# Attention: VectorE's statistics, sums over heads and softening put between the steps of a batch's matrix

## The reference, cut to what matters

```python
q = _split_heads(x @ Wq + bq)
v = _split_heads(x @ Wv + bv)
q = jax.nn.softmax(q, axis=-1) * s
k = jax.nn.softmax(q, axis=-2) * s
ctx = jnp.einsum('bhnd,bhne->bhde', k, v)
attn = jnp.einsum('bhnd,bhde->bhne', q, ctx)
attn = attn.transpose(0, 2, 1, 3).reshape(B, N, D)
return attn @ Wo + bo
```

## Time and profile before

| | |
|---|---|
| median of 3 runs | 1755.51 us (1755.17 to 1757.69) |
| the profiled execution, its own time | 1755.51 us |
| its span, first to last instruction | 1752.8 us |
| busy over the span | TensorE 90%, VectorE 64%, ScalarE 50%, GpSimd 43% |
| attention | about 787 to 967 us |
| the three matrices of batches 0, 1 and 2 | from about 848, 892 and 933 us |

### The profile page before, as it was taken

The page is one execution under the profiler, slowest core; times in us unless marked ns, Lnnn a source line. Parts: engine busy times, 40 slices in busy tenths (PEclk is TensorE's granted clock), DMA queues, the critical chain, the costliest instruction groups (busy, mean ns, idle before and its releaser), DMA issues.

```text
span 1752.8 us, 40278 instructions
## 1 busy us (share of the span) xinstructions
PE 1586.2 (90%) x14505; PEld 1252.3 (71%) x14505; DVE 1129.1 (64%) x2523; ACT 885.1 (50%) x1624; POOL 755.7 (43%) x611
## 2 busy tenths in 40 slices
PE   5649999999999999976899764999999999999997
PEld 4536878787877878764788653687878787777876
DVE  7898484858576574626788788746374645556461
ACT  5645454544444454527676564445454544544452
POOL 7403525344443426036666650452534444342503
PEclk9999999999999999997999755999999999999999
DMA  8754616263443525038777460452615243443502
GB/s 266 255 156 125 137 42 133 54 137 57 110 75 92 91 76 92 4 44 192 163 158 160 128 224 5 125 106 62 136 51 120 67 111 67 96 76 87 85 7 31
DMA packets 276544, 184.12 MB, mean 105 GB/s; under 512 B 175339, under 2 KB 263157, under 8 KB 276469
## 3 DMA queue, kind: packets, MB, share of 16 engines
q1 hardware_dynamic: 245748, 140.50, 29.6%
q0 software_dynamic: 30720, 42.62, 16.0%
HBM read 91.04 MB, written 55.06 MB: 83 GB/s over the span
## 4 chain that ended last, share of the span: by engine, by line
PE 78%; DVE 10%; ACT 3%; issue 3%; POOL 3%; DMA 3%; SPq 1%; DVEq 0%; POOLq 0%; ACTq 0%
PE bank L1637 48%; PE bank L1649 24%; ACT xt L763 2%; PE bank L1615 1%; PE bank L1583 1%; DVE bank L338 1%; DMA xs<-x_d 1%; DVE xn L1046 1%; PE bank L1690 1%; DVE xn L1135 1%; POOL rows L530 1%; PE bank L1525 1%; POOL w_d L540 1%; POOL unit_buf L535 1%; PE bank L1722 1%
## 5 line engine op out<-in xcount | busy, mean ns | idle before, releaser
L1637 PE MATMUL bank<-xT,rows 128*128 128x320 f16 x3072 | 500.5, 299 | 1.0 <-DVE w_u L1025 1.0
L1637 PE MATMUL bank<-xT,w_u 128*128 128x320 f16 x3072 | 500.8, 299 | 0.0
L1262 DVE SCALAR_TENSOR_TENSOR unit_buf<-bank,sc_cur,unit_buf 128x320 f32<-128x320 f32 x512 | 281.9, 551 | 327.3 <-PE bank L1637 318.6
L812 ACT ACTIVATE unit_buf<-bank,sc_cur 128x320 f32<-128x320 f32 x512 | 269.5, 526 | 375.4 <-PE bank L1637 373.2
L1649 PE MATMUL bank<-w_d,xs 128*128 128x256 f16 x3840 | 421.8, 273 | 0.0
L1649 PEld LDWEIGHTS bank<-w_d,xs 128*128 128x128 f16 x3840 | 375.7, 98 | 44.3
L1637 PEld LDWEIGHTS bank<-xT,w_u 128*128 128x128 f16 x3072 | 300.6, 98 | 116.7
L1637 PEld LDWEIGHTS bank<-xT,rows 128*128 128x128 f16 x3072 | 291.6, 98 | 109.6 <-issue 2.0
L460 POOL DMA_INDIRECT gat<-rows_d,id_next x160 | 183.3, 1146 | 311.1 <-issue 253.9
L1268 DVE TENSOR_TENSOR xs<-unit_buf,xs 128x320 f16<-128x320 f32 x512 | 246.9, 482 | 2.2
L818 ACT ACTIVATE xs<-unit_buf 128x320 f16<-128x320 f32 x512 | 235.6, 460 | 10.4 <-DVE unit_buf L1262 10.4
(11 more groups left out here) (238 smaller groups left out, 1618.7 us busy)
## 6 DMA issues: line engine op xcount, KB each, us to landing
rows_d<-rows SPq DMA_DIRECT2D x32, 512.0 KB, 3.7
raw_gu<-in_L_ffn_wg SPq DMA_DIRECT2D x16, 1024.0 KB, 6.7
raw_gu<-in_L_ffn_wu SPq DMA_DIRECT2D x16, 1024.0 KB
raw_d<-in_L_ffn_wd SPq DMA_DIRECT2D x16, 1024.0 KB, 5.2
x_d<-xs SPq DMA_DIRECT2D x1, 8192.0 KB, 32.8
out_x<-xs SPq DMA_DIRECT2D x16, 512.0 KB, 3.5
xs<-in_L_attn_x SPq DMA_DIRECT2D x7, 1024.0 KB, 7.4
xs<-x_d SPq DMA_DIRECT2D x6, 1024.0 KB, 6.4
```

Source lines behind the costliest of these rows:

```text
L812: act.activation(act_s[:, u % 2, :], bank[u % 2][:, 0:CW], ACT.Silu, scale=sc_cur[:, 3:4]).then_inc(S.s_ready, 1)
L1262: dve.scalar_tensor_tensor(h32[:, u % HB, :], bank[2 + u % 2][:, 0:CW], sc_cur[:, 4:5], act_s[:, u % 2, :], mult, mult).then_inc(S.h32_rea ...
L1637: mm = pe.matmul(bank[2 * m + u % 2][:, 0:CW], wgu[m][:, w, k, f * P:(f + 1) * P], xT[:, a * KD + k, c * CW:(c + 1) * CW], start=(j == 0 a ...
```

## The change

In VectorE's order of the group that makes a matrix, the three steps of the pipeline go to other places between the steps of the matrix: `stats` from behind `m2_out` to ahead of `m2_ctx`, `sum_heads` from behind `m2_top` to behind `m2_ctx`, and `soften` from behind `m2_scale` to ahead of it. Nothing is added or removed, and no other engine's order changes.

```diff
+                    chain = m is not None and j == 0
                     if now:
                         center(*now)
-                    if m is not None and j == 0:
+                    if chain:
                         m2_sums(m)
-                        m2_ctx(m)
-                        m2_out(m)
                     if far:
                         stats(*far)
-                    if m is not None and j == 0:
-                        m2_top(m)
+                    if chain:
+                        m2_ctx(m)
                     if done and j == 1:
                         finish(done[0], 0)
                     if now:
                         sum_heads(*now)
-                    if m is not None and j == 0:
-                        m2_scale(m)
+                    if chain:
+                        m2_out(m)
+                        m2_top(m)
                     if now:
                         soften(*now)
-                    if m is not None and j == 0:
+                    if chain:
+                        m2_scale(m)
                         m2_lo(m)
```

## The result

| | before | after |
|---|---|---|
| median of 20 runs each | 1756.45 us | 1760.2 us |
| lowest to highest | 1754.03 to 1758.49 | 1757.48 to 1762.45 |
| ratio, with its 95% interval | | 1.0019 (1.0013 to 1.0025) |
| span of the profiled execution | 1752.8 us | 1755.9 us |

By the ratio the changed kernel is slower by 0.19%, 3.3 us, where 3.2 us were forecast. The interval is wholly above 1, from 2.3 to 4.4 us; the ratio lies just inside the bound of 0.2%, and the two medians, 3.75 us apart, just outside it. (The 1755.51 us given ahead as the profiled execution's own time are the median of the first three runs. In all runs the time lies 1.7 to 1.8 us over the execution's span, so the 2.7 us "around the span" compare two executions. The forecast is a difference, and doesn't hang on them.)

The account below looks back on a forecast made before the run. VectorE (100.4 of 119 us busy) and TensorE (107.5) were both taken as close to full in the attention stage. The sum +4.6 - 1.3 - 0.1 = +3.2 us gave 1758.7 us, 8-in-10 range 1756.3 to 1761.0.

Parts of the forecast that it names:

- The statistics wait for x's load with the context behind them: First matrix, VectorE: statistics stand until the load lands at 855.36, so the context starts 6.64 us late; 3.0 us lost at full clock.
- TensorE comes back at half clock: First matrix: after a 7.2 us gap TensorE restarts at 1.2 GHz for 3.0 to 4.6 us; L1739 takes 2.07, not 1.13 us.
- The term: First matrix's whole loss, load wait and half clock together: 4.2 to 5.0 us, 4.6 taken as the middle.
- The second matrix wins 1.27: Second matrix: statistics fill the gap before the context, L1435 at 901.59 instead of 902.86; 1.27 us won on VectorE, 0.9 on TensorE.
- The third wins 0.1, as TensorE holds it: Third matrix: L1435 0.5 us earlier on VectorE, but TensorE gains only 0.1 us; ends 0 and 0.5.
- Nothing between the matrices: Between matrices VectorE stays the later engine, TensorE having 1.05 us to spare, so the first matrix's loss carries over whole.
- the loss is over 3.5 us: Rival: half clock until the spread is done, or later matrices give nothing; +4.1 to +5.0 us; chance 0.32.
- TensorE's idle time decides alone: Rival: the whole 6.64 us delay of TensorE's first product is lost, less 1.0 in the others; +5.6 us; chance 0.06.
- Faster: Rival: all 7.4 us of waits around the context filled, 1748.1 us, if the load has landed at 849.2; chance 0.03.

Follow-up runs that it names:

- e5_spin: Changed kernel plus 22 idle TensorE matmuls behind L1732 of the first matrix, filling the gap ahead of L1740; ratio to the kernel before 1.0013.
- e8_spin_split: Changed kernel plus idle TensorE matmuls in the first matrix's gap, 16 at once and 6 after x's last load landed; ratio to the kernel before 1.0008.
- e10_exact_before: Kernel before, old order, with the statistics' wait split: four loads at the first group, all seven two groups on; ratio to the kernel before 1.0000.
- e4_early_before: Kernel before, old order, with the last four loads of x made three larger ones, the last issued earlier; ratio to the kernel before 1.0015.
- e3_early_after: Changed kernel with the last four loads of x made three larger ones, the last issued earlier; ratio to the kernel before 1.0002.
- e9_exact_after: Changed kernel with the statistics' wait split: four loads at the first group, all seven two groups on, no load moved; ratio to the kernel before 0.9983.
- e1_stats_back: Changed kernel with the statistics put back behind the maxima, the other two moves kept; ratio to the kernel before 0.9996.

## Why the prediction was right

- *The statistics wait for x's load with the context behind them.* Shown. L1413 started 1.50 us behind the landing (forecast 1.49), at 857.15 (856.85, and the load 0.29 later). The wait was 3.96 us where 6 were forecast, because L1439 came 3 us later in this execution; in e5_spin and e8_spin_split it came at 848.4 and 848.7 and the wait was 5.91 and 5.98.
- *TensorE comes back at half clock.* Shown, with 2.07 us for L1740 as forecast and 3.0 us at 1.2 GHz, the lower of the two values taken from before. The turn was forecast for 861.5 to 862.2 and came at 861.62. The gap was forecast at about 7 us and was 4.57, again because L1439 came late. The term: 4.6 taken, 4.2 to 5.0 as its range, 4.17 measured, just below it. The price by the Trainium skill (TensorE: Matmul & The Clock Gate, HAM oscillation — how this bites in real kernels), half of the throttled time, is 1.5 us for these 3.0 and 3.2 for e5_spin's 6.5; measured were at most 1.0 and 2.6. In these two executions it bounds the cost from above; VectorE isn't waiting for all of TensorE's work there.
- *The second matrix wins 1.27.* 1.30 measured; the new waits were 0.25, 0.36 and 0.79 us, forecast 0.2, 0.3 and 0.8.
- *The third wins 0.1, as TensorE holds it.* L1435 came 0.54 us earlier against L1439 (forecast 0.51), and 0.21 of it was left at the end.
- *Nothing between the matrices.* Not quite: 0.32 us between the first and second, with a wait of 0.28 for the queries. e10_exact_before and e4_early_before, with the old order, have the same wait, and e3_early_after and e8_spin_split, with the new, don't, so it isn't the change's. It goes with TensorE's wait for the transposed rows just ahead: 1.15 us here and 1.28 in e10_exact_before, 0.96 before and 0.84 and 0.76 in the two without. Why that wait varies stays open.
- *The rivals.* That the loss is over 3.5 us is out by its mechanisms (the half clock ended after 3.0 us, and the second matrix gave its 1.30), but not by its size: the interval goes from 2.3 to 4.4 us. That TensorE's idle time decides alone is out: the context was 6.9 us later and L1435 4.5. "Faster" failed at the point it named, the load's landing; where the wait for it is gone (e9_exact_after), the kernel is 2.5 to 3.0 us faster than before, near the 2.7 us that the rival gave for that case. That includes whatever before's own wait for the load costs in the mean, which the 2.7 leave out.

So the mechanism was right, and the sum in each term to within 0.5 us. That the total is right to 0.1 is luck: the first matrix cost 0.4 less than taken, and the later landing and the way to the second matrix, 0.29 and 0.32, were in no term. And the 3.3 us are themselves known only to about 1 us.

## What to carry to other kernels

Before a step is moved ahead of another on an in-order queue, look at what it waits for in each iteration, the first above all: the same move won 1.3 us in the second matrix and lost 4.2 in the first, on a wait that had been mostly covered by the steps now behind it. And ask whether the wait is for the data that is read: here a shared count asked for three loads too many, and making it exact turned a loss of 3.3 us into a gain of 3.0 (by the ratios to before). Issuing the loads sooner was the worse cure, as they met the transposes.

## What the runs showed of the hardware

The length of the last idle stretch alone doesn't tell whether TensorE falls to half clock. The granted clock was 0.50 at the restart or within 1 us of it after 4.57 us (the changed kernel), 3.24 (e5_spin), 2.14 (e3_early_after, L1691 at 847.82) and 1.92 (e1_stats_back, L1693 at 844.16), and stayed at 1.00 after 2.20 and 0.77 (e8_spin_split) and after 2.67 (the changed kernel, L1691 at 834.19). Nor does it tell how long the half clock lasts: 3.0 us behind the 4.57, 6.5 behind the 3.24. So filling part of an idle stretch, as e5_spin does, gave no safety in its trace; that it is worse than leaving the stretch empty isn't shown, since in e5_spin's execution L1439 came 2.9 us earlier than in the changed kernel's.

The same transpose of queries took 6.52 and 6.30 us beside a 1.5 MB load, and 3.29 to 4.86 in the eleven traces where it ran beside a 1 MB one.
